# Mixture-of-experts kernel: the second product takes gelu rows and their remainders as one moving block, and a body of 192 columns is added

## What is computed

```
logits = tokens @ gate_weight.T               # 2048 tokens, 8 experts
top1 = argmax(logits); probs = softmax(logits)
rank = position of the token among those of its expert
kept = rank < 320                             # capacity C
hmid = gelu(dispatch[e] @ wi[e])              # (320 x 512) @ (512 x 2048)
eout = hmid @ wo[e]                           # (320 x 2048) @ (2048 x 512)
out[token] = probs[token, e] * eout[e, rank]  # 0 for tokens that aren't kept
```

## Time and profile before

| | us |
|---|---|
| median of 3 runs (1098.29 to 1100.72) | 1098.69 |
| span of the profiled execution, first to last instruction | 1094.0 |
| TensorE busy | 1046.3 |
| VectorE busy | 720.6 |
| ScalarE busy | 543.8 |
| GpSimd busy | 144.0 |

### The profile page before, as it was taken

How to read it: one execution, slowest core, us unless ns; L and a number is a source line. 1 busy time by engine, 2 the same in 40 slices (tenths; PEclk the granted TensorE clock), 3 DMA queues, 4 the chain that set the end, 5 groups by cost and what they waited for, 6 DMA issues and landing times.

```text
span 1094.0 us, 20943 instructions
## 1 busy us (share of the span) xinstructions
PE 1046.3 (96%) x7924; PEld 988.2 (90%) x7924; DVE 720.6 (66%) x1089; ACT 543.8 (50%) x851; POOL 144.0 (13%) x138
## 2 busy tenths in 40 slices
PE   9699999999999999599999996999999999999995
PEld 6599999999999999478777776999999999999995
DVE  8556565776577686478786765557777777665552
ACT  5445455565556565253342324455665656554441
POOL 3201111203021110100000022002212021120101
PEclk9899999999999999899999998999999999999998
DMA  8568546566464761500011235436566575664410
GB/s 309 176 242 302 187 171 216 183 219 206 162 232 160 251 208 39 178 1 1 1 39 39 79 116 176 154 117 244 206 228 211 190 244 188 230 208 145 164 39 25
DMA packets 83276, 177.32 MB, mean 162 GB/s; under 512 B 4192, under 2 KB 4704, under 8 KB 83168
## 3 DMA queue, kind: packets, MB, share of 16 engines
q1 hardware_dynamic: 75488, 152.61, 40.5%
q0 software_dynamic: 7168, 23.07, 5.9%
q10 hardware_dynamic: 576, 1.05, 0.3%
HBM read 162.04 MB, written 18.87 MB: 165 GB/s over the span
## 4 chain that ended last, share of the span: by engine, by line
PE 91%; DVE 3%; DMA 2%; issue 1%; ACT 1%; POOL 1%; POOLq 0%; SPq 0%; ACTq 0%; DVEq 0%
PE psH L1223 13%; PE psH L1222 13%; PE psH L1224 13%; PE acc L1230 12%; PE acc L1231 12%; PE acc L1229 12%; PE acc L1222 3%; PE acc L1223 3%; PE acc L1224 3%; PE psT L1446 1%; PE acc L1402 1%; PE psH L1402 1%; DVE row_stats L829 1%; PE psT L1551 1%; PE psT L1281 1%
## 5 line engine op out<-in xcount | busy, mean ns | idle before, releaser
L1222 PE MATMUL psH<-dth,wih 128*128 128x240 f32 (+5 forms) x1024 | 294.3, 287 | 0.0
L1223 PE MATMUL psH<-dtl,wih 128*128 128x240 f32 (+5 forms) x1024 | 293.4, 287 | 0.8 <-issue 0.8
L1230 PE MATMUL acc<-htl,woh 128*128 128x240 f32 (+5 forms) x1024 | 293.3, 286 | 0.0
L1231 PE MATMUL acc<-hth,wol 128*128 128x240 f32 (+5 forms) x1024 | 293.1, 286 | 0.0
L1224 PE MATMUL psH<-dth,wil 128*128 128x240 f32 (+5 forms) x1024 | 293.1, 286 | 0.0
L1229 PE MATMUL acc<-hth,woh 128*128 128x240 f32 (+5 forms) x1024 | 293.1, 286 | 0.0
L796 DVE TENSOR_TENSOR wol<-raw_wo,woh 128x1024 fp32r<-128x1024 f32 x128 | 155.6, 1222 | 146.6 <-ACT woh L613 146.6
L647 ACT ACTIVATE gel<-psH 128x320 f32<-128x320 f32 x256 | 112.1, 438 | 189.1 <-PE psH L1224 183.9
L613 ACT ACTIVATE woh<-raw_wo 128x1024 fp32r<-128x1024 f32 x128 | 134.2, 1056 | 132.2 <-PE acc L1231 132.1
L1223 PEld LDWEIGHTS psH<-dtl,wih 128*128 128x128 f32 x1024 | 193.0, 188 | 1.1 <-issue 1.1
L1222 PEld LDWEIGHTS psH<-dth,wih 128*128 128x128 f32 x1024 | 192.9, 188 | 0.4
(11 more groups left out here) (194 smaller groups left out, 1147.9 us busy)
## 6 DMA issues: line engine op xcount, KB each, us to landing
raw_wi<-in_wi SPq DMA_DIRECT2D x64, 1024.0 KB, 5.1
raw_wo<-in_wo SPq DMA_DIRECT2D x64, 1024.0 KB, 5.5
out_x<-xt SPq DMA_DIRECT2D x4, 1024.0 KB, 5.9
xt<-in_x SPq DMA_DIRECT2D x6, 512.0 KB, 8.0
xt<-x SPq DMA_DIRECT2D x3, 1024.0 KB, 10.2
raw_u<-in_wuT SPq DMA_DIRECT2D x1, 1024.0 KB, 10.9
raw_u<-in_wvT SPq DMA_DIRECT2D x1, 1024.0 KB, 12.6
xt<-in_x ACTq DMA_DIRECT2D x2, 256.0 KB, 3.6
```

The lines of the kernel that those rows point to most:

```text
L1222: pe.matmul(out, lh, rh, start=first, stop=False)
L1223: pe.matmul(out, lh, rl, start=False, stop=False)
L1230: pe.matmul(out, lh, rl, start=False, stop=False, skip_group_check=True)
L1231: return pe.matmul(out, ll, rh, start=False, stop=False, skip_group_check=True)
```

## The change

The rows hth and htl of one tile now stand beside each other in one buffer ht. For widths up to JOINT = 256 the helper onto sends both as one moving block of 2w columns against the high weights, and writes the remainder's products to the upper half of the bank, columns 256 and up; the third matmul is as before. For wider bodies onto sends the same three matmuls as before. So that both halves are added, after ACT's copy of acc[c] VectorE adds acc[c][:, 256:512] times a factor joint to eoT[:, c, 0:256], for each expert; joint is 1 for an expert with at most 256 tokens and 0 otherwise. What waited for ACT's copy (eoT_done) on TensorE waits for this sum (eoT_sum). WIDTHS gets a body of 192 before 240. Four banks are cleared whole at the start, and clear_acc writes zeros.

```diff
-WIDTHS = range(240, CAP + 1, 16)
+WIDTHS = (192, 240, 256, 272, 288, 304, 320)
+JOINT = 256
-VISITED = (2, 6)
+VISITED = (2, 7)
...
-        hth = put("hth", [P, 2, ICS, CAP], F32R)
-        htl = put("htl", [P, 2, ICS, CAP], F32R)
+        ht = put("ht", [P, 2, ICS, 2, CAP], F32R)
+        hth, htl = ht[:, :, :, 0, :], ht[:, :, :, 1, :]
...
-            pool.iota(least[:, :, :], [[0, E], [WIDTHS.step, NW - 1]], base=WIDTHS.start, channel_multiplier=0,
-                      allow_small_or_imprecise_dtypes=True).then_inc(pool_const, 1)
+            for k, w in enumerate(WIDTHS[:-1]):
+                ins = pool.memset(least[:, :, k:k + 1], float(w))
+            ins.then_inc(pool_const, 1)
...
-                        act.activation(eoT[:, c, :], acc[c][:, 0:CAP], copy).then_inc(s.eoT_done, 1)
+                        act.activation(eoT[:, c, :], acc[c][:, 0:CAP], copy).then_inc(s.eoT_copied, 1)
...
+                then(dve.tensor_scalar(joint[:, :], ps_taken, JOINT + 0.5, None, ALU.is_lt))
...
+                then(dve.tensor_copy(joint_now[:, 0:1], joint[:, 0:1]))
...
-            for bank in (*acc[2:], *psH):
+            dve.memset(nil[:, :], 0.0)
+            for bank in acc[:2]:
+                dve.memset(bank[:, JOINT:], 0.0).then_inc(banks_set, 1)
+            for bank in acc[2:]:
+                dve.memset(bank[:, :], 0.0)
+            for bank in psH:
                 ins = dve.memset(bank[:, 0:CAP], 0.0)
...
+                    dve.tensor_copy(joint_now[:, 1 - a:2 - a], joint[:, bass.ds(e + 1, 1)])
...
+                    for c in range(DC):
+                        dve.wait_ge(s.acc_done, DC * (PAIRS * e + PAIRS) + c + 1)
+                        dve.wait_ge(s.eoT_copied, DC * e + c + 1)
+                        dve.scalar_tensor_tensor(eoT[:, c, 0:JOINT], acc[c][:, JOINT:], joint_now[:, side:side + 1],
+                                                 eoT[:, c, 0:JOINT], ALU.mult, ALU.add).then_inc(s.eoT_sum, 1)
                     if not last:
                         for c in range(DC):
                             tokens(e + 1, c)
...
-            def onto(out, lhs, rhs):
+            def onto(bank, w, lhs, both):
 
-                (lh, ll), (rh, rl) = lhs, rhs
-                pe.matmul(out, lh, rh, start=False, stop=False, skip_group_check=True)
-                pe.matmul(out, lh, rl, start=False, stop=False, skip_group_check=True)
-                return pe.matmul(out, ll, rh, start=False, stop=False, skip_group_check=True)
+                lh, ll = lhs
+                if w <= JOINT:
+                    pe.matmul(bank.rearrange("p (r q) -> p r q", r=2)[:, :, 0:w], lh, both[:, :, 0:w],
+                              start=False, stop=False, skip_group_check=True)
+                else:
+                    for r in range(2):
+                        pe.matmul(bank[:, 0:w], lh, both[:, r, 0:w], start=False, stop=False, skip_group_check=True)
+                return pe.matmul(bank[:, 0:w], ll, both[:, 0, 0:w], start=False, stop=False, skip_group_check=True)
...
+                pe.wait_ge(banks_set, 2)
...
-                            pe.wait_ge(banks_set, 1)
+                            pe.wait_ge(banks_set, 3)
...
-                        pe.matmul(acc[c][:, 510:512], ones[:, :], ones[:, 0:2], start=True, stop=True)
+                        pe.matmul(acc[c][:, 510:512], ones[:, :], nil[:, :], start=True, stop=True)
...
-                        pe.wait_ge(s.eoT_done, DC * e + c + 1)
+                        pe.wait_ge(s.eoT_sum, DC * e + c + 1)
...
-                    if j >= 1:
-                        peek(1)
+                    peek(1)
```

More of the change, by code:

```diff
@@ L138, in build_kernel @@
         digit = put("digit", [P, E], F32)
+        joint = put("joint", [P, E], F32)
+        joint_now = put("joint_now", [P, 2], F32)
+        nil = put("nil", [P, 2], BF16)
         code8 = put("code8", [P, E], F32)
@@ L258, in __init__ @@
                 self.acc_done = sem(f"acc_done{n}")
-                self.eoT_done = sem(f"eoT_done{n}")
+                self.eoT_sum = sem(f"eoT_sum{n}")
+                self.eoT_copied = sem(f"eoT_copied{n}")
                 self.tokT_done = sem(f"tokT_done{n}")
@@ L537, in _ @@
                 act.sem_inc(s.gelu_done, ICS)
-                act.sem_inc(s.eoT_done, DC)
                 def norm(g, rstd_sem, xn_sem, tiles=GROUP):
@@ L962, in _ @@
                 dve.sem_inc(s.out_dve, 3)
+                dve.sem_inc(s.eoT_sum, DC)
                 if n == 0:
@@ L1431, in mm2 @@
                             d = slice(c * P, (c + 1) * P)
-                            ins = onto(acc[c][:, 0:w], (woh[:, k, j, d], wol[:, k, j, d]),
-                                       (hth[:, k, j, 0:w], htl[:, k, j, 0:w]))
+                            ins = onto(acc[c][:, :], w, (woh[:, k, j, d], wol[:, k, j, d]), ht[:, k, j])
                         if k == 1:
@@ L1459, in turn_last @@
                     for c in range(DC):
-                        pe.wait_ge(s.eoT_done, DC * E + c + 1)
+                        pe.wait_ge(s.eoT_sum, DC * E + c + 1)
                         for k, bank in HELD:
```

## The result

The changed kernel takes 1119.41 us (median of 4 runs, 1115.62 to 1119.83) where the kernel before took 1098.49 on the same chip: ratio 1.0203, 95% interval 1.0179 to 1.0227. It is slower by about 2%; the prediction was 1091.0, a gain, so even the sign is wrong. The profiled span is 1113.9 against 1094.0, 19.9 more; the mean granted clock 0.974 against 0.983.

A forecast was written before the change was run, and what follows sets the result against it. The tensor engine, busy 96% of the span, was taken as the bound. Gain 14.2 us from the merge, less 5.3 for sums and 1.2 inside the 192 body, makes 7.7: 1098.7 to 1091.0 us, own range 1087 to 1096.

The forecast's parts named there:

- At nothing: List of items taken to cost 0, among them start memsets, branch tests, visits and the 192 body's first use (bounds 0 and 1.1 us).
- a head that grows by over 0.9 us: At the start of an expert: one of the signs that would show the forecast wrong.
- something else slower: Leftover case for an unnamed cause that makes the kernel slower; no size given, chance 0.02.
- The visits, at nothing: Visits to bodies ahead of the layers' loops were taken to add no time.
- The merge: Expert's second product: two matmuls of w columns become one of 2w; gains 12.5, 1.3 and 0.4 us, together 14.2.
- my line of columns: Spacing of matmul starts taken as 0.453 ns a column: 175.3 ns at 384 columns, 218.8 at 480.
- The loads: 192 body's narrower matmuls: weight loads keep the pace at 112 ns, so no gain; bound 24.6 us of gain.
- the rival that they don't bind: 192 body: loads don't set the pace at 192 columns; up to 24.6 us more gain less some 6, 1072; chance 0.06.
- The two runs: Joint matmul's moving block and output: two runs cost nothing; rival of a fixed part each, 1095.2 us, chance 0.13.
- The sums: VectorE's added sums between experts: 0.38 us after 240, 0.68 after 192, 0.05 after wide bodies, 0.42 at layer ends; 5.3 in all.
- Inside the 192 body: Last pair of steps: the gelu remainder htl comes late, 0.3 us in each of four experts, 1.2 us cost.
- The slower rival: Sums between experts don't hide: 1.4 us at each of 14 boundaries, 7.4 us slower, 1106; chance 0.10.

The follow-up runs named there:

- after_2_6: The changed kernel with six visits to bodies ahead of the second layer in place of seven, the one to the 320 body left out: 1112.5 us, ratio 1.0164.
- before_and_body: The kernel before, without merge or sums, plus a seventh body of 224 columns and one more visit in the second layer: 1114.07 us, ratio 1.0166.
- one_run: no_body_256 with the joint moving block and its output as one run of 2w columns each, so the output differs: 1092.23 us, ratio 0.9962.
- no_sums: no_body_256 without VectorE's added sums, so the remainder's products don't reach the output of joint bodies: 1085.11 us, ratio 0.9885.
- no_body_256: The changed kernel without the 256 body, so six bodies, and six visits in the second layer in place of seven: 1091.07 us, ratio 0.9974.
- merge_alone: The changed kernel's merge and sums with the six widths of the kernel before, no 192 body, visits 2 and 6: 1093.98 us, ratio 0.9976.
- visits_3: no_body_256 with three visits in the second layer in place of six: 1100.87 us, ratio 1.0041.
- five_bodies: The changed kernel with five bodies (192, 240, 272, 288, 320) and visits 2 and 5: 1099.7 us, ratio 1.0032.
- unused_body: The kernel before with a seventh body of 248 columns that no expert runs at: 1124.61 us, ratio 1.0252.
- after_3_visits: The changed kernel with three visits ahead of the first layer's loop in place of two: 1117.52 us, ratio 1.019.

## Why the prediction was wrong

- **The step that failed** is the one under "At nothing": "The 192 body is one more to be used first; bounds 0 and 1.1, I take 0". The row that I leaned on showed one late body, and I took it for the price of a first use. The price of an added body isn't paid by that body. It moves all that lie behind it, and they were paid for again and again: five heads longer by 2.7 to 3.7 us in the first layer, where 192 is never used (15.0 in all), some 2.7 at the lower clock behind them, 7.8 from the last expert of the layer through the mixer and the visits, and 1.9 at one more head. Nor was the row a first use: the 240 body had been visited ahead of that layer, and yet the branch to it took 2.52 us in the trace before, with two instruction packets at the time. It was already a block that had been displaced and came a second time. What would have warned: the instruction packets in the DMA view, none in the stretch of six experts before. That says the kernel stood where all its code was kept; I read the view for data alone. The prediction did name the sign to look for, a head that grows by over 0.9 us, but gave it no mechanism and no chance beyond the 0.02 of "something else slower".
- **"The visits, at nothing"**, in the same sentence, failed by the same cause. The seventh visit alone is not to blame (after_2_6), though some of the 7.8 us may be its own.
- **The merge**: forecast 331 and 287 ns for joint plus third at 240 and 192, measured 327 and 287.5. The sum is right, in part by luck: at 192 it splits into 200 + 87.5 and not 175 + 112. The start behind the joint matmul comes 25 ns later than by my line of columns, and the one behind the third 25 ns earlier than by the pace of the loads that I had put there. Why the two differences cancel isn't shown.
- **The loads** set 111 to 112 ns at 192 columns in the first product, and at 224 in before_and_body. Right there, and the rival that they don't bind is out; behind a joint matmul they don't set the pace (87.5 ns). The rule of the Trainium skill weighed in the prediction (TensorE: Matmul & The Clock Gate, Back-to-back issue gap), 82.5 ns, which that section gives for a matmul by itself, has the rows of the first product at 192 columns against it.
- **The two runs**: no cost (one_run). Right.
- **The sums**: forecast 0.38 after a 240 body and 0.68 after a 192 body; PE's transposes come 0.46 and 0.78 after the last matmul's start in place of 0.1, some 0.35 and 0.65 late. The head is 0.06 longer. Over the boundaries no_sums gives 0.5 at 240 and up to 0.13 where I had 0.05 at wide ones. One sum takes 0.48 where I had 0.41:

```profile
L1083 DVE SCALAR_TENSOR_TENSOR eoT<-acc,joint_now,eoT 128x256 f32<-128x256 f32 x64 | 27.8, 478 | 7.6 <-ACT eoT L685 7.5
```

- **Inside the 192 body**: 40.0 to 40.1 us from first to last start. The measured spacings make 192 x 0.112 + 64 x 0.2875 = 39.9, so 0.1 to 0.2 is left for waits where I had 0.3.
- **The slower rival** I priced, sums that don't hide, has the right sign and the wrong cause: 1106 by a wait on DVE of 1.4 us a boundary, which is nowhere. Nearly all of the 0.13 for slower stood on causes that the runs don't show.

Where the first layer doesn't wait, the change is worth what no_body_256 shows, 4.5 us by the medians, where its own sum is 7.7 less 2.7 for the expert that goes from 256 to 272: 5.0.

**What is open.** The two conditions, a first dispatch that hits and a reach of at most seven blocks, tell all kernels of the table apart, but they are read off it, not derived, and they hold for layer one alone. In layer two the second expert waits in most of the kernels (not in merge_alone and before_and_body), and the seventh in visits_3 and five_bodies, which have no more than six bodies. Which block gives way isn't settled either. It is not simply the oldest of seven. In the changed kernel the 240 body, by the table's reckoning all in block 2, is fetched for the fourth expert and again for the sixth. The DMA view at the fourth expert's branch, from there to the sixth's, and at the sixth's:

```profile
q8 instruction: 2, 0.03, 2.2%
q8 instruction: 2, 0.03, 0.1%
q8 instruction: 2, 0.03, 2.0%
```

At most three packets lie between the two fetches of that block. No run placed code by absolute address. unused_body and before_and_body, both with seven wide bodies, have equal profiled spans (1111.7 and 1112.2), so what makes the other four executions of unused_body 9 to 13 us longer stands in no trace.

## What to carry to other kernels

Code is a resource with a size and a place. Before adding a variant of a loop body, a branch target or an unrolled copy to the engine that bounds the kernel, count the instruction packets of its queue in a steady stretch: if there are none, the kernel sits inside what is kept, and it isn't known by how much; lay the new body behind those that the loop needs first, and compare the packets after. A body that isn't run can cost 2.5%, and an idle wait of 3 us can cost again, by a lower clock behind it.

## What the runs showed of the hardware

- TensorE's instruction queue moves 16 KB a packet (0.69 MB in 42). A branch at an expert's head to a block that isn't there, or is still on its way, takes 2.2 to 6.5 us in these traces, against some 0.2 to one that is there. The Trainium skill (Advanced Engine Details and Errata, ISA Cache) gives 128 KB on TensorE in lines of 16 KB or 256 instructions, which would be eight; the packet size agrees. That eight are kept no run shows: no_body_256 keeps the five blocks that it goes round, 0 and 2 to 5 by the table's reckoning, through six experts; kernels that reach block 7, or miss at the first dispatch, fetch some of theirs again. The same section's line that only two such lines exist doesn't hold for this engine: no_body_256 fetches nothing from 106 to 400 us while it goes round over these five. Runtime: NRT & Kernel Launch of the same skill (Instruction fetch mechanics) says that a taken branch to a target outside what is held waits for a fetch; this is what the waits show.
- Blocks that were displaced include the one with the loop's own head (after_3_visits: the jump back takes 5.32 us and PE idles for 3.60).
- After an idle stretch of some 3 us on a PE that had been busy throughout, the granted clock was at the lower level for the first matmuls of some bodies of the changed kernel (third and sixth expert, idle 3.42 and 2.67 us) and not of others (fourth and fifth, idle 2.84 and 2.73). What decides wasn't tried.
